# Attention output stored by query and gathered by head in the reload, and two value loads one step earlier

## The chip, the cores and the metric

The kernel runs on one core of one Trainium2 chip. The metric is the device time of one execution in microseconds (us), as the median of several runs. The engines are named as the profile names them: PE is TensorE (PEld its weight loads), DVE is VectorE, ACT is ScalarE, POOL is GpSimd, SP is SyncE, and SPq or ACTq is the sequencer of that engine, which also issues DMAs.

## The reference, cut to what matters

A decoder layer on 64 sequences of 64 tokens with 128 features, float32: self-attention, cross-attention, and a feed-forward part with one shared expert and one of seven routed ones.

```python
p = einsum('bsd,ed->bse', layernorm(x), Wv) + bv       # q = k = v = p, 16 heads of 8
out = softmax(q @ k.T / sqrt(8)) @ v                   # (b, h, s, 8)
out = out.reshape(b, s, h * dk)                        # heads are NOT transposed back
x = x + einsum('bsd,ed->bse', out, Wo) + bo
x = x + cross_attention(layernorm(x), ctx, ctx)        # no projections
x = x + ffn(layernorm(x))                              # shared and routed experts
```

What matters here is the third line. The output of the self-attention has the order (head, query, feature) for a sequence, and it is read again as 64 rows of 128 numbers. A row therefore holds the 8 features of 16 successive queries of one head: row 4h + j has head h and queries 16j to 16j + 15. The kernel's partitions hold queries, with all heads side by side, so this regrouping crosses partitions. The kernel makes it by writing the output to a scratch tensor in DRAM, `attention_out`, and reading it back.

## The kernel before, in words

The 4096 tokens are cut into U = 32 units of 128 tokens, two sequences (b = 0, 1) each. The first phase is a software pipeline over steps t = 0 to 38. In step t the table `LAG` (L223) gives each stage its unit: norm and transposition for unit t, projection and self scores for t - 1, self softmax for t - 2, the stage `out` for t - 3, the stage `q` (output projection, then the cross query and cross scores) for t - 4, cross softmax for t - 5, and so on. `phase_a` (L235) calls each engine's `body` for each step. Steps 0 to 4 have orders of their own (`opening`), and after step 32 every engine but SP has an order written out by hand. The second phase runs the feed-forward part.

The way of the self-attention's output of unit u:

- DVE divides by the softmax sums in `normalise("s", u)` (L1484 to L1491), which writes `on_s` and raises `s_on`. From the second unit on it first waits until both stores of the unit before have landed (`s_out`).
- Two DMAs store it, `store_half` (L283): SP stores sequence 0 (L338), ACT sequence 1 (`second_store`, L1133). Both raise `s_out`. In ACT's order the store stands behind both exponentials of the self softmax (L1250 to L1256), which wait for DVE's subtractions (L1474).
- SP waits for `s_out` of both and issues one reload of 128 rows of 512 bytes into `orow` (L350). It raises `w_rows0` or `w_rows1`, by the unit's parity.
- PE waits for that in `turn_output` (L766), which is the first operation of PE's step u + 4 (L851), and transposes the rows (L771). ACT copies the result (L1181), PE projects it (L776). The last but one unit (30) goes through `turn_last_row` (L894) in the order written out by hand; the last unit needs no way through DRAM.

In one step SP issues, in this order: store, `last_values` in step 33 alone, up to two fills of the routing scratch (`prefill_of_step`, 130 KB each, steps 6 to 31), reload, at most one load of weights, and four loads of cross keys (up to step 31). ACT issues its store, one bulk load in many steps, and two loads of cross values (`cross_values`, L1138) with `ring` slot u % 8 as their target. A load of values moves 64 rows into pieces of 32 bytes, as a store of the attention output does. `last_values` (L327) issues from SP the four value loads of units 30 and 31.

Of the kernel before, what the change touches and what calls it, by code (L numbers as in the profile page):

```python
# [22 lines left out]
P = 128  # L23
D = 128
S = 64
B = 64
H = 16
DK = D // H
NB = P // S
U = B // NB  # L30
# [29 lines left out]
F32 = mybir.dt.float32  # L60
# [6 lines left out]
def build(nc, x, ctxk, ctxv, wv, bv, wo, bo, rw, rb, wup, wdn, ident, hmask, tri, small, tokens, out):  # L67
    ctx = ExitStack()
    with ctx:
# [5 lines left out]
        def sem(name):  # L75
            if name not in sems:
                sems[name] = ctx.enter_context(nc.semaphore(name))
            return sems[name]
# [192 lines left out]
        block = ctx.enter_context(nc.Block())  # L271


        o_dram = nc.dram_tensor("attention_out", (U, NB, H, S, DK), F32, kind="Internal").ap()
        o_rows = o_dram.rearrange("u b h q d -> (u b h q d)").rearrange("(u p c) -> u p c", p=P, c=D)
        hs_dram = nc.dram_tensor("sorted_rows", (SLOTS * P, ROW), F32, kind="Internal").ap()
        hs_halves = hs_dram.rearrange("r (k c) -> (r k) c", k=2)
        hs_tiles = hs_dram.rearrange("(s p) c -> p s c", p=P)
# [3 lines left out]

        def store_half(eng, u, b):  # L283

            load(eng, o_dram[u, b, :, :, :].rearrange("h q d -> q h d"),
                 on["s"][S * b:S * (b + 1), :, :, :].rearrange("p a c d -> p (a c) d"), "s_out")

        @block.sync
        def _(sp):
# [45 lines left out]
            def body(t, u, live):  # L335
                if live("out") and u["out"] < U - 1:
                    sp.wait_ge(sem("s_on"), at(u["out"]))
                    store_half(sp, u["out"], 0)  # L338
                if t == U + 1:
                    last_values(U - 2)  # L340
                    last_values(U - 1)
                for tile in prefill_of_step(t):
                    load(sp, hs_tiles[:, tile, :], nowhere_row[:, :], "prefilled")
                if 6 <= t < 6 + P // H:
                    load(sp, wo_turn[H * (t - 6):H * (t - 5), :, :], wo.rearrange("(q d) e -> q d e", d=DK), "l_turn")
                if live("out") and u["out"] < U - 1:
                    sp.wait_ge(sem("s_out"), 16 * NB * at(u["out"]))
                    if u["out"] >= 2:
                        sp.wait_ge(sem("s_oT"), at(u["out"]) - 2)
                    load(sp, orow[u["out"] % 2][:], o_rows[u["out"], :, :], f"w_rows{u['out'] % 2}")  # L350
                weights_of_step(t)
                for q, half in key_parts(t):
                    keys(t // CHUNK, q, half)
                if t == CHUNK - 1:
                    load(sp, x_all[:, RING:RING + 4, :], xv[:, RING:RING + 4, :], f"l_x{RING}")
                if t == U - 4:
                    load(sp, rb_sb[:], rb.partition_broadcast(P), "l_router")
                if t == U - 3:
                    load(sp, small_sb[:], small.partition_broadcast(P), "l_router")
                if t == U - 2:  # L360
                    load(sp, tok_sb[:], tokens, "l_router")
# [294 lines left out]
        def _(pe):  # L656
# [106 lines left out]

            def turn_output(u):

                pe.wait_ge(sem(f"w_rows{u % 2}"), 16 * (u // 2 + 1))  # L766
                if u == 0:
                    pe.wait_ge(sem("obias"), 1)
                if u >= 1:
                    pe.wait_ge(sem("x_q"), u)  # L770
                nc.tensor.transpose(ps_oT, orow[u % 2][:], id_sb[:]).then_inc(sem("s_oT"), 1)  # L771
# [121 lines left out]

            def turn_last_row(u):  # L894

                pe.wait_ge(sem(f"w_rows{u % 2}"), 16 * (u // 2 + 1))
                nc.tensor.transpose(ps_oT, orow[u % 2][:], id_sb[:]).then_inc(sem("s_oT"), 1)

            def cross_scores_last():
# [1044 lines left out]
```

## Time and profile before

| | us |
|---|---|
| median of 3 runs | 407.66 |
| lowest and highest run | 405.99, 408.55 |
| time of the profiled execution | 406.13 |
| span of the profile in it | 403.9 |

The granted clock of PE is 0.998 of full speed over the span. The profiled execution's own time is 2.2 us more than its span, which is what lies around the program's first and last instruction. A line of the profile names a group of instructions by its line in the code, its engine, its operation and the tiles out<-in.

### The profile page before, as it was taken

How to read it: one execution, taken by the hardware profiler on the slowest of the kernel's cores; microseconds unless marked ns; L12 is line 12 of the kernel's file. 1: busy time of each engine (PE TensorE's matmuls, PEld its weight loads, DVE VectorE, ACT ScalarE, POOL GpSimd, SP SyncE). 2: the span in 40 equal slices, each digit the busy share in tenths (PEclk: the TensorE clock that was granted, in tenths of full speed). 3: DMA queues.
4: the chain of work that ended last, by engine and by line, in shares of the span. 5: the costliest groups of instructions: out<-in, count | busy, mean ns of one | idle time of the engine just before them, and what ended most of it. 6: DMA issues, size and time to landing. Idle time of an engine off the chain costs nothing.

```text
span 403.9 us, 16288 instructions
## 1 busy us (share of the span) xinstructions
PE 393.0 (97%) x5549; PEld 309.9 (77%) x5550; DVE 308.4 (76%) x847; ACT 295.8 (73%) x684; POOL 283.2 (70%) x476
## 2 busy tenths in 40 slices
PE   8989999999999999999999899899999999999996
PEld 5556666666666666666666667799999999999996
DVE  6759999999999999999999786864444454455444
ACT  7568999999999999999999766432224666666651
POOL 8756888888888888888888734467777454444442
PEclk9999999999999999999999999999999999999999
DMA  6254656777777777766554500012223454520001
GB/s 93 59 82 61 99 93 98 138 108 136 111 141 117 125 119 137 137 119 104 68 65 51 54 2 3 0 61 87 87 86 108 111 135 136 138 82 21 30 33 54
DMA packets 176325, 35.22 MB, mean 87 GB/s; under 512 B 145587, under 2 KB 174646, under 8 KB 176256
## 3 DMA queue, kind: packets, MB, share of 16 engines
q1 hardware_dynamic: 71296, 21.43, 24.7%
q10 hardware_dynamic: 102144, 6.81, 16.2%
q0 software_dynamic: 2816, 6.10, 4.3%
q8 instruction: 40, 0.66, 0.7%
q14 instruction: 29, 0.24, 0.2%
HBM read 20.86 MB, written 15.67 MB: 90 GB/s over the span
## 4 chain that ended last, share of the span: by engine, by line
PE 84%; DVE 5%; DMA 4%; issue 2%; ACT 2%; SPq 1%; POOL 1%; ACTq 0%; DVEq 0%; POOLq 0%
PE psum L919 21%; PE psum L672 14%; PE psum L681 14%; PE psum L1026 11%; PE psum L693 9%; PE psum L703 3%; PE psum L771 2%; DMA orow<-attention_out 2%; PE psum L803 2%; PE psum L776 2%; PE psum L810 1%; PE psum L660 1%; PE psum L1068 1%; SPq L198 1%; DVE mx_s L1454 1%
## 5 line engine op out<-in xcount | busy, mean ns | idle before, releaser
L1713 DVE TENSOR_TENSOR gT<-gT,psum 128x384 f32<-128x384 f32 x66 | 36.6, 554 | 65.8 <-ACT gT L1356 40.7
L460 POOL TENSOR_TENSOR k_s<-pT,hmask_sb 128x1024 f32<-128x1024 f32 x32 | 60.9, 1902 | 16.2 <-issue 14.7
L1356 ACT ACTIVATE gT<-psum 128x384 f32<-128x384 f32 x70 | 34.1, 487 | 45.2 <-PE psum L919 36.2
L633 POOL DMA_INDIRECT out<-yrow,token x38 | 37.0, 973 | 40.1 <-DVE yrow L1848 35.4
L1026 PE MATMUL psum<-wdn_sb,gT 128*128 (+1 forms) x420 | 58.3, 276 | 0.7 <-POOL gT L607 0.6
L919 PE MATMUL psum<-fhT,wtile 128*128 128x128 f32 x456 | 57.1, 275 | 0.0
L919 PEld LDWEIGHTS psum<-fhT,wtile 128*128 128x128 f32 x456 | 53.9, 192 | 0.0
L1026 PEld LDWEIGHTS psum<-wdn_sb,gT 128*128 128x128 f32 x420 | 52.4, 192 | 1.3 <-POOL gT L607 1.0
L919 PE MATMUL psum<-hT_all,wup_sb 128*128 128x128 f32 x384 | 48.1, 276 | 1.0 <-ACT gT L1356 1.0
L1454 DVE TENSOR_REDUCE mx_s<-psum 128x16 f32<-128x1024 f32 x33 | 40.4, 1225 | 9.1 <-PE psum L672 6.0
L919 PEld LDWEIGHTS psum<-hT_all,wup_sb 128*128 128x128 f32 x384 | 45.4, 192 | 1.2 <-ACT gT L1356 1.2
L681 PEld LDWEIGHTS psum<-id_sb,pr_x 128*128 128x128 f32 x248 | 27.3, 141 | 24.1 <-ACT pr_x L1118 23.7
L1118 ACT ACTIVATE pr_x<-pr_x,rs 128x512 f32<-128x512 f32 x60 | 40.4, 715 | 3.4 <-DVE pr_x L1466 2.3
L1474 DVE TENSOR_TENSOR pr_s<-psum,mx_s 128x512 f32<-128x512 f32 x64 | 41.8, 658 | 0.0
L1118 ACT ACTIVATE pr_s<-pr_s 128x512 f32<-128x512 f32 x64 | 40.2, 631 | 2.0 <-DVE pr_s L1474 1.7
L1125 ACT COPY prT_s<-psum 128x512 f32<-128x512 f32 x66 | 36.4, 586 | 2.5
L681 PE MATMUL psum<-id_sb,pr_x 128*128 128x128 f32 x248 | 37.4, 280 | 0.5 <-ACT pr_x L1118 0.5
L681 PE MATMUL psum<-id_sb,pr_s 128*128 128x128 f32 x264 | 36.8, 279 | 0.4 <-ACT pr_s L1118 0.3
L1474 DVE TENSOR_TENSOR pr_x<-psum,mx_x 128x512 f32<-128x512 f32 x58 | 37.1, 681 | 0.0
L1125 ACT COPY prT_x<-psum 128x512 f32<-128x512 f32 x62 | 36.7, 595 | 0.1
L1459 DVE TENSOR_REDUCE mx_x<-psum 128x8 f32<-128x512 f32 x56 | 36.0, 685 | 0.4 <-PE psum L672 0.3
L1385 ACT COPY wtile<-wup_sb 128x704 f32 x38 | 29.6, 778 | 7.7 <-issue 7.1
(193 smaller groups left out, 866.9 us busy)
## 6 DMA issues: line engine op xcount, KB each, us to landing
sorted_rows<-nowhere_row SPq DMA_DIRECT2D x38, 130.0 KB, 3.4
ring<-sorted_rows SPq DMA_DIRECT2D x30, 130.0 KB
wup_sb<-in_wup SPq DMA_DIRECT2D x14, 176.0 KB, 2.6
orow<-attention_out SPq DMA_DIRECT2D x31, 64.0 KB
ring<-in_ctxv ACTq DMA_DIRECT2D x60, 32.0 KB, 3.8
cross_keys<-in_ctxk ACTq DMA_DIRECT2D x14, 128.0 KB, 3.3
ring<-cross_keys SPq DMA_DIRECT2D x112, 16.0 KB
rows_all<-in_x ACTq DMA_DIRECT2D x10, 128.0 KB, 3.3
```

Of the source, the lines that this page charges most:

```text
L460: nc.gpsimd.tensor_tensor(k_s[:], pT[:].rearrange("p (b k) -> p b k", b=NB).unsqueeze(2).broadcast_to([P, NB, HG, S]), hmask_sb[:, 0:HG].u ...
L633: pool.indirect_dma_start(out=out, out_offset=bass.IndirectOffsetOnAxis(ap=token[p][:, 0:1], axis=0), in_=yrow[p][:, :], in_offset=None, b ...
L672: last = nc.tensor.matmul(ps_s[k][g][S * b:S * (b + 1), :], q[S * g:S * (g + 1), S * b:S * (b + 1)], keys[S * g:S * (g + 1), b, :, :].rear ...
L681: last = nc.tensor.transpose(ps_s[k][g][:, i * P:(i + 1) * P], pr[k][:, g, 2 * i:2 * i + 2, :].rearrange("p h k -> p (h k)"), id_sb[:])
L693: last = nc.tensor.matmul(ps_wT[k][VW * i:VW * (i + 1), g, S * b:S * (b + 1)], values[:, VW * pair:VW * (pair + 1)], prT[k][:, g, i, S * b ...
L919: return nc.tensor.matmul(ps[p][:, c * P:(c + 1) * P], weights[:, start:start + P], tokens, start=True, stop=True)
L1026: last = nc.tensor.matmul(ps_y[p], gT[place_of(n) if isinstance(n, int) and n < FIRST else p][:, c, :], wdn_sb[:, expert, c, :], start=(c ...
L1118: nc.scalar.activation(pr[k][:, g, :, :], pr[k][:, g, :, :], ACT.Exp, scale=rs[u % 2][:, 0:1] if k == "x" else float(DK) ** -0.5).then_inc ...
L1125: nc.scalar.copy(prT[k][:, g, :, :].rearrange("p i q -> p (i q)"), ps_s[k][g]).then_inc(sem(f"{k}_prT"), 1)
L1454: nc.vector.tensor_reduce(mx[k][:], both(k), AX.X, ALU.max).then_inc(sem(f"{k}_mx"), G)
L1474: nc.vector.tensor_tensor(pr[k][:, g, :, :], scores_of(k, g), mx[k][:, g, :].unsqueeze(2).broadcast_to([P, HG, S]), ALU.subtract).then_inc ...
L1713: nc.vector.tensor_tensor(g, g, ps_up[k][:, 0:CH * P], ALU.mult).then_inc(sem("f_g"), 1)
```

## The change

Three edits. First, `attention_out` gets the order (unit, sequence, query, head, feature). A store then writes 64 rows of 512 bytes, where it wrote 1024 pieces of 32 bytes. Second, the reload becomes two DMAs on SP, one for each sequence, each of which gathers 1024 pieces of 32 bytes; a piece is 8 features of one head and one query, and the 16 pieces of a row lie 512 bytes apart in DRAM. Both raise the same semaphore, so PE waits for twice the count. Third, `last_values` for units 30 and 31 is issued in step 32, behind the reload, where it was issued in step 33, ahead of the reload.

```diff
@@ -271,8 +271,7 @@
-        o_dram = nc.dram_tensor("attention_out", (U, NB, H, S, DK), F32, kind="Internal").ap()
-        o_rows = o_dram.rearrange("u b h q d -> (u b h q d)").rearrange("(u p c) -> u p c", p=P, c=D)
+        o_dram = nc.dram_tensor("attention_out", (U, NB, S, H, DK), F32, kind="Internal").ap()
@@ -282,8 +281,8 @@
         def store_half(eng, u, b):
 
-            load(eng, o_dram[u, b, :, :, :].rearrange("h q d -> q h d"),
-                 on["s"][S * b:S * (b + 1), :, :, :].rearrange("p a c d -> p (a c) d"), "s_out")
+            load(eng, o_dram[u, b, :, :, :].rearrange("q h d -> q (h d)"),
+                 on["s"][S * b:S * (b + 1), :, :, :].rearrange("p a c d -> p (a c d)"), "s_out")
@@ -336,9 +335,6 @@
-                if t == U + 1:
-                    last_values(U - 2)
-                    last_values(U - 1)
                 for tile in prefill_of_step(t):
@@ -347,7 +343,12 @@
-                    load(sp, orow[u["out"] % 2][:], o_rows[u["out"], :, :], f"w_rows{u['out'] % 2}")
+                    for b in range(NB):
+                        load(sp, orow[u["out"] % 2][S * b:S * (b + 1), :].rearrange("p (i d) -> p i d", d=DK),
+                             o_dram[u["out"], b, :, :, :].rearrange("(j i) h d -> h j i d", i=H), f"w_rows{u['out'] % 2}")
+                if t == U:
+                    last_values(U - 2)
+                    last_values(U - 1)
                 weights_of_step(t)
@@ -763,7 +764,7 @@ and @@ -893,7 +894,7 @@
-                pe.wait_ge(sem(f"w_rows{u % 2}"), 16 * (u // 2 + 1))
+                pe.wait_ge(sem(f"w_rows{u % 2}"), 16 * NB * (u // 2 + 1))
```

## Rows read from the trace of the kernel before

**Rows 1.** The page, busy time of each engine and granted clock in 40 slices.

```profile
PE 393.0 (97%) x5549; PEld 309.9 (77%) x5550; DVE 308.4 (76%) x847; ACT 295.8 (73%) x684; POOL 283.2 (70%) x476
...
PEclk9999999999999999999999999999999999999999
```

**Rows 2.** Busy time by stretch: stretch, its us, busy of each engine, clock, DMA share.

```profile
5.90:33.00 27.10, 24.71 (x331) 14.51 (x329) 18.31 (x38) 16.16 (x39) 17.40 (x26) 1.00 0.51 77
...
46.90:224.80 177.90, 177.84 (x3329) 119.53 (x3329) 173.73 (x464) 168.46 (x414) 155.77 (x288) 1.00 0.67 109
224.80:258.00 33.20, 30.05 (x367) 22.30 (x363) 25.36 (x71) 22.45 (x47) 13.24 (x30) 1.00 0.14 15
```

**Rows 3.** The chain that ended last, one steady step: start us, us, what.

```profile
190.91 0.26 PE psum L771
...
196.73 1.02 PE psum L672 x8
197.75 0.26 PE psum L771
```

**Rows 4.** Timeline of a steady step: start us, us, engine, line, operation, tiles.

```profile
189.51 0.28 DVE L1490 TENSOR_TENSOR on_s<-psum,rden_s 128x128 f32<-128x128 f32 x1
189.70 0.68 DVE L1474 TENSOR_TENSOR pr_s<-psum,mx_s 128x512 f32<-128x512 f32 x1
...
190.42 0.64 ACTq L198 DMA_DIRECT2D attention_out<-on_s  x1
190.44 0.58 SPq L198 DMA_DIRECT2D attention_out<-on_s  x1
...
192.90 0.64 ACTq L198 DMA_DIRECT2D ring<-in_ctxv  x1
```

**Rows 5.** Timeline of the next stretch, SP and DVE.

```profile
194.51 0.35 SPq L198 DMA_DIRECT2D orow<-attention_out  x1
194.96 1.34 SPq L198 DMA_DIRECT2D ring<-cross_keys  x4
...
196.35 0.28 DVE L1490 TENSOR_TENSOR on_s<-psum,rden_s 128x128 f32<-128x128 f32 x1
```

**Rows 6.** Waits of 46.9 to 224.8: who waited for whom, us in total, times, longest.

```profile
PEld psum L771 <- DMA orow<-attention_out: 11.4, 14, 0.8
PEld psum L771 <- issue: 9.7, 12, 0.8
...
SPq L198 <- DMA attention_out<-on_s: 54.1, 26, 3.0
```

**Rows 7.** DMA issues, KB each, median us from issue to landing; the whole span.

```profile
wup_sb<-in_wup SPq DMA_DIRECT2D x14, 176.0 KB, 2.6
...
ring<-in_ctxv ACTq DMA_DIRECT2D x60, 32.0 KB, 3.8
...
out<-rows_all SPq DMA_DIRECT2D x2, 64.0 KB, 1.6
```

**Rows 8.** The same of 100 to 200 alone.

```profile
ring<-in_ctxv ACTq DMA_DIRECT2D x30, 32.0 KB, 4.1
```

**Rows 9.** Packets by DMA queue (q1 is SP's, q10 ACT's), 226.2 to 228.2.

```profile
q1 hardware_dynamic: 2238, 0.07, 60.8%
```

**Rows 10.** Packets by DMA queue, 129.2 to 130.6, then 194.4 to 195.4.

```profile
DMA packets 2563, 0.08 MB, mean 61 GB/s; under 512 B 2563, under 2 KB 2563, under 8 KB 2563
...
q10 hardware_dynamic: 608, 0.02, 30.3%
```

**Rows 11.** SP from 217 on, timeline.

```profile
217.18 0.58 SPq L198 DMA_DIRECT2D attention_out<-on_s  x1
220.88 0.35 SPq L198 DMA_DIRECT2D orow<-attention_out  x1
223.53 0.58 SPq L198 DMA_DIRECT2D attention_out<-on_s  x1
224.16 3.57 SPq L198 DMA_DIRECT2D ring<-in_ctxv  x4
```

**Rows 12.** The chain at 227.8, then the timeline with PE's idle time before the line.

```profile
227.85 3.73 DMA orow<-attention_out
...
231.71 0.30 PE L897 MATMUL psum<-id_sb,orow 128*128 128x128 f32 x1 [0.88 <-DMA orow<-attention_out]
```

**Rows 13.** Timeline of the opening, then a piece of the chain there.

```profile
20.07 0.66 ACTq L198 DMA_DIRECT2D attention_out<-on_s  x1
...
26.44 0.33 PE L771 MATMUL psum<-id_sb,orow 128*128 128x128 f32 x1 [0.90 <-DMA orow<-attention_out]
...
29.98 2.94 DMA orow<-attention_out
```

More of the change, by code:

```diff
@@ L894, in turn_last_row @@
             def turn_last_row(u):
-                pe.wait_ge(sem(f"w_rows{u % 2}"), 16 * (u // 2 + 1))
+                pe.wait_ge(sem(f"w_rows{u % 2}"), 16 * NB * (u // 2 + 1))
                 nc.tensor.transpose(ps_oT, orow[u % 2][:], id_sb[:]).then_inc(sem("s_oT"), 1)
```

## The prediction

> **What bounds the kernel now.** I read the page first, then the busy time by stretch, the chain of waits in one step, the timeline of that step, the waits of PE and SP, and last the DMA issues and packets. The page shows PE busy for 393.0 of 403.9 us at full granted clock [rows 1]. By stretch the reader is to see that this isn't an average over slack: from 46.9 to 224.8, 26 steps of 6.84 us, PE is busy for 177.84 of 177.90 us, while the DMA engines are busy for 0.67 of the time [rows 2]. The chain of a steady step is PE alone, and PE's transposition of the reloaded rows (L771) starts at 190.91 and 197.75, 6.84 us apart, right behind the cross scores (L672) [rows 3]. So nothing that the change makes faster can shorten a steady step; it can only lengthen one, if the rows come after PE wants them. What is to gain lies outside: at the first transposition PE is idle for 0.90 us waiting for the reload [rows 13], and at unit 30 for 0.88 us [rows 12]. Together 1.8 us, that is all.
>
> **How much cover the way through DRAM has.** DVE's output ends at 189.51 + 0.28 = 189.79 [rows 4], and PE takes the rows of that unit at 197.75 [rows 3]: 7.96 us. Let D be the time from DVE's end to the landing of the reload; as long as D is under 7.96, the step stays. Before the change the stores go out at 190.42 and 190.44 [rows 4] and SP issues the reload at 194.51 [rows 5], 4.1 us later. The reload's landing is in the chain twice, 2.94 us after its issue [rows 13] and 3.73 us [rows 12]; so D before is up to 4.72 + 2.94 = 7.7, and the waits agree that it is close: in 14 of 26 steps the rows came after PE had finished its last weight load, which is at most 0.8 us ahead of the transposition [rows 6]. That idle time is PEld's, under the running L672, and costs nothing now.
>
> What a miss costs: after a transposition at 190.91 the output that ends at 196.35 + 0.28 = 196.63 [rows 5] belongs to the unit two further on. A unit's round is thus two steps, 5.72 + D, and a step takes (5.72 + D) / 2 once D is over 7.96. A D that is 0.3 us too long costs 0.15 us a step, 4 us over 27 steps.
>
> **Part 1, the store.** ACT's store can't go out earlier: it stands behind the second exponential, which waits for the subtraction that ends at 189.70 + 0.68 = 190.38 [rows 4]. So the later issue stays at 0.6 us behind DVE's end. No row has a store of 64 rows of 512 bytes in this traffic. The nearest are the stores of 128 such rows at the end of the program with nothing beside them, 1.6 us to landing, and the 176 KB weight loads inside the traffic, 2.6 us [rows 7]. I take the middle, 2.1; with 0.6 the reload is issued at 2.7 behind DVE's end, where it was at 4.7. SP's wait for the store, 54.1 us over 26 steps [rows 6], 2.1 each, about disappears; nothing else is late for it, since the key loads behind it have a whole step.
>
> The Trainium skill, "DMA: Bandwidth & Descriptors", section "Specifications", says that below 512 bytes a DMA engine does a read-modify-write. By this rule the store loses a penalty and the reload gets it, for the same 2048 pieces a unit; the rule agrees with a change that moves cost rather than removing it.
>
> **Part 2, the reload.** One issue of 0.35 us becomes two of about 0.6, as the stores and value loads of 1024 pieces take [rows 4]. SP has room for it: in rows 5 it ends its keys at 196.30 with the reload at 194.51; with the reload two us earlier it is done before the next store. For the landing, the nearest row is the load of values, also 1024 pieces of 32 bytes from DRAM to SBUF: 3.8 us to landing over the span [rows 7], 4.1 us in the busiest part [rows 8]. The second gather follows in the same queue. In SP's queue four value loads in a row moved 2238 packets in 2.0 us, 1119 a us [rows 9], so the second lands 1024 / 1119 = 0.9 us behind the first. With 3.8 and 4.1 the pair needs 4.7 to 5.0. D after is 2.7 + 4.7 = 7.4, or 7.7 in the busiest part: as before, and under 7.96 by 0.2 to 0.5. The median leaves room, the single steps not all: I count one step in four as late by 0.2, which costs half of that each, 7 x 0.1 = 0.7 us.
>
> The bounds of the pair: below, as many packets as two queues moved together, 2563 in 1.4 us or 1831 a us [rows 10], so 3.8 - 0.9 + 2048 / 1831 = 4.0 us and D = 6.7, no step late. Above, a value load that runs alone with 608 packets in 1.0 us [rows 10], so 4.1 + 1024 / 608 = 5.8 us, D = 2.7 + 5.8 = 8.5, a miss of 0.54, 0.27 x 27 = 7.3 us. That a piece is now read apart from its neighbours, 512 bytes on, is in no row of the trace. I stay with the value loads in SP's queue, rows 9, for they are the same queue and size.
>
> On the two queues becoming one: the row shows 1119 a us from one queue and 1831 a us from two. The Trainium skill, "DMA: Bandwidth & Descriptors", section "Issuing engines are not separate DMA queues", has it that issuing from several engines saves only the sequencer's time. By this rule the pair would land 0.7 us earlier, D = 6.7 and the steady part would cost nothing; the rows speak against it.
>
> **Part 3, the last values.** In step 33 the four value loads take SP's queue from 224.16 for 3.57 us, up to 227.73, and the reload goes out at 227.85 behind them [rows 11, 12]. Moved, they follow the reload pair of unit 29: store at 217.18, ACT's 0.6 behind, pair issued at 219.8 to 221.1, values to 221.1 + 3.6 = 224.7. The store of unit 30 wants to go at 223.53 [rows 11] and now goes at 224.7, and its queue still holds packets: 6 x 1024 from 221.2 + 1.2 at 1119 a us end at 227.9, at 1831 at 225.8. The store lands 0.4 behind that or 2.1 behind its issue, 226.8 to 228.3; I take 227.6. With little beside it (DMA share 0.14, [rows 2]) the pair takes 4.2, between 4.0 and 4.7, and lands at 231.8, where the old reload landed at 227.85 + 3.73 = 231.58 [rows 12]. So the move takes 3.57 us of issues off the chain and gets nothing for it: the longer reload eats it. I take +0.2, between -0.9 (PE's idle time gone) and +1.4 (store at 228.3, pair 4.7).
>
> **The opening.** Unit 0: ACT's store goes at 20.07 [rows 13], lands at 22.2, the pair at 26.9 with 4.7, where PE started at 26.44. The 256 KB load behind the old reload now comes after the pair. Unit 1: stores at 26.45, landing 28.5, pair 33.2 or 32.5 with 4.0, against 29.98 + 2.94 = 32.92. I take +0.3 for both, between -0.9 and +1.0.
>
> **Sum.** 0.7 + 0.2 + 0.3 = +1.2 us. Against the profiled execution's 406.1 us (span 403.9 and 2.2 around it) that is 407.3. The median of the runs is 407.7, 1.5 above the profiled one, so for a median I say 408.9 (407.7 + 1.2).
>
> **The rivals.** A, the gather outlasts its cover (slower): scattered reads of 32 bytes in one queue beside ACT's value loads. Its place is the wait of L771 in every steady step. It decides from a pair longer than 7.96 - 2.7 = 5.3 us; at the upper bound of 5.8 it costs 7.3 us, with the 0.5 of the ends 407.7 + 7.8 = 415.5. For it: no row has reads that lie apart, the cover has 0.2 to 0.5 us left, and ACT's value loads (192.90, [rows 4]) fall beside the gather. Against it: DMA engines are idle for a third of the time [rows 2].
> B, a small gain: the store lands in 1.6 and the pair in 4.0. Then both idle times of PE shrink, together at most -1.8 us: 405.9 in the median, 404.3 for the profiled one. Against it: the pair's price.
> C, the end alone is worse: values and gather in one queue hold back the store of unit 30, +1.4 there, and the opening +1.0, with the steady part 0.7: +3.1, 410.8. For it: the four issues now stand in front of a store that the chain runs through.
>
> **How the numbers follow.** The forecast has 0.43, A 0.27, B 0.16, C 0.14. A measurement of this kernel can tell about 1% (4.1 us) from no change. Forecast, B and C lie within it, A over it except for its mildest part (0.02); I leave 0.03 for a gain over 1%, which no row offers, taken from B. So faster 0.03, same 0.71, slower 0.26. The range goes from B's 405.9 to A's 415.5, rounded up to 416.
>
> **What would show it.** Right: SP's reload goes out about 2.1 us behind the later store, L771 stays 6.84 us apart, PE is busy for all of the steady stretch, and the idle time before L897 is near 0.9. Wrong: idle time of PE (not only PEld) before L771 in most steps, the steady stretch longer than 178 us, or cross scores no longer directly ahead of L771 in the chain. If the store still takes 4 us with its 512-byte rows, its cost was traffic and not its pieces, and D goes to 9.4 and the kernel to some 427.

## The result, and the profile after

The changed kernel takes 422.91 us (median of 4 runs, 420.66 to 425.35), the one before 407.13 us in the same session (405.99 to 408.55). The ratio is 1.039, with a 95% interval of 1.034 to 1.045: slower, beyond the upper end of the range. The profiled execution took 420.66 us, span 418.4.

The page of the kernel after, busy time, clock, two of the queues and the chain's shares:

```profile
PE 397.1 (95%) x5549; PEld 312.8 (75%) x5550; DVE 308.8 (74%) x847; ACT 297.1 (71%) x684; POOL 283.8 (68%) x476
...
PEclk9989999999999999999999969999999999999999
...
q1 hardware_dynamic: 101552, 21.43, 26.9%
q10 hardware_dynamic: 72384, 6.81, 12.6%
...
PE 54%; DMA 21%; SPq 15%; DVE 3%; issue 3%; ACT 2%; POOL 1%; DVEq 0%; POOLq 0%; ACTq 0%
```

Beside [rows 1], PE has 4.1 us more of busy time and 14.5 us more of span. Two slices have a lower clock, which had none before. The chain is now DMA and SP's sequencer (SPq) for 36% of the span.

Busy time by stretch, the kernel after; columns as in [rows 2]:

```profile
5.90:33.00 27.10, 23.59 (x294) 14.68 (x293) 15.47 (x32) 15.01 (x35) 16.47 (x25) 0.94 0.47 72
...
46.90:224.80 177.90, 170.12 (x3215) 114.69 (x3217) 166.42 (x446) 161.94 (x398) 148.88 (x273) 1.00 0.65 108
```

PE was busy for 177.84 us of the steady stretch [rows 2] and is now for 170.12. The DMA engines are no busier than they were (0.65, before 0.67), so by this mean it isn't their throughput that ran out.

Waits of 46.9 to 224.8, kernel after:

```profile
PEld psum L772 <- DMA orow<-attention_out: 28.0, 24, 2.6
...
PE psum L772 <- DMA orow<-attention_out: 7.7, 10, 1.8
```

The second line is the loss; before there was no such line [rows 6]. The steady chain of [rows 3] was PE alone. After, from 142 to 151 us (start, us, what):

```profile
142.22 3.18 DMA attention_out<-on_s
145.40 0.02 issue
145.42 0.55 SPq L198
145.97 0.04 issue
146.01 4.27 DMA orow<-attention_out
150.28 0.04 issue
150.32 0.33 PE psum L772
```

Ahead of 142.22 the chain runs twice through seven SPq pieces and the landing of a store, from 128.13 to 135.18 and on to 142.22, 7.05 and 7.04 us. So the circle store, landing, reload pair, weights, keys, next store on SP sets the pace. One turn of it in the timeline of SP, kernel after:

```profile
159.37 1.47 SPq L198 DMA_DIRECT2D orow<-attention_out  x2
160.88 1.64 SPq L198 DMA_DIRECT2D wdn_sb<-in_wdn  x1
162.56 2.88 SPq L198 DMA_DIRECT2D ring<-cross_keys  x4
165.49 0.47 SPq L198 DMA_DIRECT2D attention_out<-on_s  x1
```

And the output that this store carries, from the timeline of all engines:

```profile
162.65 0.28 DVE L1491 TENSOR_TENSOR on_s<-psum,rden_s 128x128 f32<-128x128 f32 x1
163.57 0.51 ACTq L198 DMA_DIRECT2D attention_out<-on_s  x1
```

DVE ends at 162.93 and ACT stores its half 0.64 later, as forecast. SP stores its half 2.56 us after DVE's end. In the kernel before, the turn of the same unit has its reload at 152.58, the weight load at 152.95 (0.43 us) and the keys at 153.43 (1.45 us); SP was done at 154.88, DVE at 155.53, and the store went out at 155.56. The next turn of the kernel before, which is at the time of the one above:

```profile
160.73 0.33 SPq L198 DMA_DIRECT2D orow<-attention_out  x1
161.10 0.44 SPq L198 DMA_DIRECT2D wdn_sb<-in_wdn  x1
161.58 2.68 SPq L198 DMA_DIRECT2D ring<-cross_keys  x4
164.30 0.58 SPq L198 DMA_DIRECT2D attention_out<-on_s  x1
```

The weight load's issue took SP 0.44 us there, and 1.64 behind the gather pair. The store of this turn was late before the change too, though: DVE's output ended at 162.37 and it went out at 164.30, 1.93 us later, behind key issues of 2.68 us. Before, that is the one late turn among units 10 to 23, the next worst being 0.92; after, eleven of the 14 are later than 1.1 us. The held weight load is no single case either. Issues in 130 to 205 by tile, first the kernel before, then after (ns min/median/max; first and last start in us):

```profile
L198 SPq DMA_DIRECT2D wdn_sb<-in_wdn x6: 428/435/441, 153.0 to 188.2; - x6
...
L198 SPq DMA_DIRECT2D wup_sb<-in_wup x3: 433/433/433, 132.9 to 146.9; - x3
```

```profile
L198 SPq DMA_DIRECT2D wdn_sb<-in_wdn x6: 661/1675/1895, 160.9 to 197.4; - x6
L198 SPq DMA_DIRECT2D wup_sb<-in_wup x4: 738/1401/1632, 132.5 to 153.7; - x4
```

Where the time went, by the start of PE's transpositions (before, then after): unit 0 26.44, then 28.11; unit 3 46.79, then 49.77; unit 29 224.81, then 235.58; unit 30 231.71, then 244.26; end of the span 403.88, then 418.41. So 3.0 us come by unit 3, 7.8 in units 4 to 29, 1.8 at unit 30 and 2.0 behind it.

The opening, chain of waits after:

```profile
22.92 5.14 DMA orow<-attention_out
28.06 0.04 issue
28.11 0.47 PE psum L772
28.58 1.71 PE psum L682 x8
```

Two stretches of the kernel after with PE's clock halved (columns as in [rows 2]):

```profile
28.00:31.40 3.40, 3.29 (x34) 2.96 (x37) 0.54 (x2) 1.71 (x4) 0.00 (x0) 0.50 0.22 30
...
243.10:249.90 6.80, 5.62 (x24) 3.31 (x25) 2.14 (x9) 1.98 (x5) 1.80 (x5) 0.50 0.14 23
```

In the first, the eight matmuls of L682 take 1.71 us, where the chain has 0.96 for eight of them at full clock. Each stretch came with a longer idle time of PE ahead of the transposition, 2.20 us and 2.66 us, than the 0.90 and 0.88 of before [rows 12, 13]. The clock fell from 2.4 to 1.2 GHz inside that idle time, 0.1 us before its end in the first and 1.2 us in the second.

The end of the phase, timeline of SP after, which answers to [rows 11]:

```profile
233.06 4.47 SPq L198 DMA_DIRECT2D ring<-in_ctxv  x4
237.58 0.67 SPq L198 DMA_DIRECT2D attention_out<-on_s  x1
240.83 1.28 SPq L198 DMA_DIRECT2D orow<-attention_out  x2
```

DVE's output of unit 30 ends at 234.27 (its row starts at 233.98 and has 0.29); SP's store waits 3.3 us for the four value issues, which the change moved ahead of it.

### The profile page after: what moved, and what is told of

Read it like the earlier page. It is cut to its first block, busy times and chain, and to the rows that moved or that the text cites. A ratio compares the mean times of both kernels' runs of the same rounds, so it can differ in the third digit from the quotient of the medians.

```text
span 418.4 us, 16319 instructions
## 1 busy us (share of the span) xinstructions
PE 397.1 (95%) x5549; PEld 312.8 (75%) x5550; DVE 308.8 (74%) x847; ACT 297.1 (71%) x684; POOL 283.8 (68%) x476
## 3 DMA queue, kind: packets, MB, share of 16 engines
q1 hardware_dynamic: 101552, 21.43, 26.9%
q10 hardware_dynamic: 72384, 6.81, 12.6%
## 4 chain that ended last, share of the span: by engine, by line
PE 54%; DMA 21%; SPq 15%; DVE 3%; issue 3%; ACT 2%; POOL 1%; DVEq 0%; POOLq 0%; ACTq 0%
PE psum L920 21%; SPq L198 15%; DMA attention_out<-on_s 14%; PE psum L1027 10%; DMA orow<-attention_out 6%; PE psum L682 5%; PE psum L673 5%; PE psum L694 4%; PE psum L661 1%; PE psum L704 1%; PE psum L1069 1%; ACT pr_s L1119 1%; PE psum L772 1%; DVE mx_s L1455 1%; PE psum L711 1%
## 5 line engine op out<-in xcount | busy, mean ns | idle before, releaser
L682 PEld LDWEIGHTS psum<-id_sb,pr_x 128*128 128x128 f32 x248 | 27.4, 141 | 23.8 <-ACT pr_x L1119 23.5
L682 PE MATMUL psum<-id_sb,pr_x 128*128 128x128 f32 x248 | 37.3, 280 | 0.5 <-ACT pr_x L1119 0.5
L682 PE MATMUL psum<-id_sb,pr_s 128*128 128x128 f32 x264 | 36.9, 281 | 0.4 <-ACT pr_s L1119 0.3
```

The lines of the kernel that those rows point to most:

```text
L682: last = nc.tensor.transpose(ps_s[k][g][:, i * P:(i + 1) * P], pr[k][:, g, 2 * i:2 * i + 2, :].rearrange("p h k -> p (h k)"), id_sb[:])
```

## The experiments

The table has means over units 10 to 23, read from the timeline and the landings of each DMA: how long after DVE's end the later store goes out, from there to the reload's issue ("lands"), the reload's issue to its landing, their sum D, and SP's time from the reload's issue to the end of the last issue of its step ("SP block"; the last key load, or the tiny loads). The step is the distance of PE's transpositions. One traced execution stands behind each row, and two of the same kernel differ by 0.15 us a step (7.38 and 7.53), so smaller differences than that say nothing. Most experiments ran on chips where the kernel before takes 420 us. The extra time, some 12 us, lies behind the attention phase: the changed kernel is at unit 30 at 244.26 in its first trace and at 247.15 in its second, and ends at 418.41 and 433.15. Why is open. So each ratio is with the kernel before on its own chip. The rows "two plain reloads" and "two in pieces" ran where it takes 408.

| kernel | ratio [95%] | later store | lands | reload lands | D | SP block | step |
|---|---|---|---|---|---|---|---|
| before | 1 | 0.78 | 3.94 | 2.39 | 7.11 | 2.52 | 6.86 |
| after | 1.039 [1.034, 1.045] | 1.62 | 2.62 | 4.44 | 8.68 | 4.47 | 7.38 |
| after, again | 1.041 [1.034, 1.048] | 1.53 | 2.44 | 4.71 | 8.68 | 4.40 | 7.53 |
| two tiny loads | 1.003 [1.000, 1.007] | 0.94 | 3.73 | 2.76 | 7.43 | 3.07 | 6.93 |
| plain reload | 0.991 [0.987, 0.996] | 0.64 | 2.45 | 2.59 | 5.68 | 2.39 | 6.85 |
| two plain reloads | 0.994 [0.990, 0.998] | 0.64 | 2.52 | 3.53 | 6.69 | 3.41 | 6.85 |
| two in pieces | 1.017 [1.010, 1.024] | 1.51 | 2.42 | 4.16 | 8.09 | 4.31 | 7.14 |
| weights late | 1.011 [1.006, 1.016] | 0.82 | 2.43 | 4.70 | 7.95 | 3.76 | 7.04 |
| mixed ways | 1.019 [1.014, 1.024] | 1.09 | 3.25 | 3.89 | 8.23 | 3.65 | 7.23 |
| stores on ACT | 1.037 [1.031, 1.043] | 1.18 | 3.16 | 4.02 | 8.36 | 4.09 | 7.35 |
| keys first | 1.024 [1.017, 1.030] | 0.64 | 3.70 | 4.48 | 8.82 | - | 7.58 |
| one gather by ACT | 1.115 [1.108, 1.121] | 0.64 | 2.41 | 3.94 | 6.99 | 2.87 | 8.30 |
| weights late, values behind | 1.006 [1.002, 1.010] | 0.69 | 2.29 | 4.66 | 7.63 | 3.23 | 6.92 |

**Parts of the change undone or done alone.** First the changed kernel with the values back in step 33, ahead of the reload.

```diff
+                if t == U + 1:
+                    last_values(U - 2)
+                    last_values(U - 1)
...
-                if t == U:
-                    last_values(U - 2)
-                    last_values(U - 1)
```

> The changed kernel with the value loads of units 30 and 31 back in step 33, ahead of the reload (third edit undone). Theory 1 (SP's sequencer is what the gathers block: DMAs issued behind the pair wait their turn, so SP's next store goes out late): in the changed kernel SP's store of unit 30 went out 3.3 us behind DVE's end, behind the four value loads. Back in step 33 it goes out within 0.6 us, but the pair then stands behind 3.6 us of value issues. Transposition 29 to 30, 8.7 us in the changed kernel and 6.9 before, becomes 7.3 to 8.2; the kernel 0.5 to 1.5 us faster than the changed one, about 421 to 422. Theory 2 (the store and the pair are themselves too long, whenever they are issued): no change of the steady part, and the end as in the changed kernel or worse, 423. Neither expects the steady part to change.

Measured 1.029 [1.025, 1.033]. Both stores of unit 30 go out within 0.39 us of DVE's end again. About 1% comes back; the rest stays, so the moved values are the smaller part. (Its traced execution, 438.23 us, was the longest of its four, so its steps aren't in the table.) Now that part alone, on the kernel before (the same lines the other way round).

> The kernel before with the third edit alone: value loads of units 30 and 31 in step 32 behind the reload. The single reload of unit 30 no longer stands behind 3.6 us of issues. Theory 1: SP's store of unit 30 goes out late instead (by about 0.5 to 1.5 us, the values end issuing at about 224.7), so of PE's 0.88 us idle at L897 about half goes; the kernel -0.5 to +0.5 against before, 407. Theory 2: nothing is late for issuing, the whole 0.88 us goes: 406.3. A result over 409 would say that the values' place makes a good part of the loss by itself.

0.9985 [0.9955, 1.0015]: no difference. The store of unit 30 goes at 1.15 behind DVE and the single reload lands in 2.00 us. The move costs only together with the gathers, whose pieces stand in the queue as well. Third, both stores issued by ACT.

```diff
-                if live("out") and u["out"] < U - 1:
-                    sp.wait_ge(sem("s_on"), at(u["out"]))
-                    store_half(sp, u["out"], 0)
...
+                store_half(act, u, 0)
```

> The changed kernel with both stores issued by ACT, one behind the other, none by SP. Theory 1: the later store goes out about 1.1 us behind DVE's end in every unit (1.6 on average and up to 2.75 in units 10 to 23 of the changed kernel), so with landing 2.6 and pair 4.4 D is 8.1 or less and steps of units 10 to 23 take 6.9 to 7.0 us where they took 7.38; the end gains too, since SP's blocked store was 3.3 us late. In all 413 to 416. Theory 2: the path is as long as before with a store half a microsecond later than the best, so steps stay at 7.3 to 7.4 and the kernel at 420 or more.

Measured 1.037 [1.031, 1.043], as the change. The store is off SP and goes out at 1.18 in every unit, as forecast, yet the gain didn't come. The landing took 3.16 us where 2.6 were expected, the second store's issue alone being 1.12, so D is 8.36. And DVE's output itself ends later: 6.07 us behind the transposition of two units before, in the mean of units 10 to 23, where the changed kernel has 5.78. The formula gives (6.07 + 8.36) / 2 = 7.2 for these; why DVE is later is open. ACT queue, timeline of this run:

```profile
160.64 0.50 ACTq L198 DMA_DIRECT2D attention_out<-on_s  x1
...
161.18 1.12 ACTq L198 DMA_DIRECT2D attention_out<-on_s  x1
```

The theory in its first form, take the store off SP and all is well, fell. Fourth, weights and keys issued ahead of the wait and the pair.

```diff
+                weights_of_step(t)
+                for q, half in key_parts(t):
+                    keys(t // CHUNK, q, half)
...
-                weights_of_step(t)
-                for q, half in key_parts(t):
-                    keys(t // CHUNK, q, half)
```

> The changed kernel with SP's loads of weights and cross keys issued ahead of the wait for the stores, so that nothing but the pair stands at the end of SP's step. Theory 1: SP's time of waiting for the store takes them, the next store goes out on time (0.0 to 0.6 us, later one 0.6), and steps of units 10 to 23 fall from 7.38 towards 6.9 to 7.1; the pair itself may land up to 1 us later behind their packets. In all 413 to 418. Theory 2: the pair lands later behind more packets and nothing is gained: 422 or more.

1.024 [1.017, 1.030]: some two fifths of the loss go, less than expected. Timeline of SP in this run, behind a pair at 162.28:

```profile
164.66 1.28 SPq L198 DMA_DIRECT2D attention_out<-on_s  x1
165.98 1.23 SPq L198 DMA_DIRECT2D sorted_rows<-nowhere_row  x2
167.25 0.46 SPq L198 DMA_DIRECT2D wdn_sb<-in_wdn  x1
167.75 1.48 SPq L198 DMA_DIRECT2D ring<-cross_keys  x4
169.32 1.50 SPq L198 DMA_DIRECT2D orow<-attention_out  x2
```

It tells more than its time. The weight load, with no pair right ahead of it, is issued in 0.46 us again. The store that follows the pair takes 1.28 here, but 0.48 in the other 13 of units 10 to 23, where up to 3.3 us lie between the pair's issue and it. The later store is on time in all 14, at 0.64. But the pair now waits for SP's own issues: 3.70 us from store to pair, for a store that lands in 2.60, so D is 8.82. The lateness has moved from the store to the pair, and in this traced execution (433.46 us, the longest of its four) the steady stretch is no better than the change's, PE being busy for 167.10 of 177.90 us. Where the gain of the median lies is not shown.

**The change again, and the queue unloaded.** First the change as it is:

> The changed kernel unchanged, as a control beside the others of this call. All theories: as on record, 1.03 to 1.05 times the kernel before; steps of units 10 to 23 at 7.3 to 7.7 us, transposition 30 at 244 to 248.

1.041 [1.034, 1.048]: the change costs the same on this chip. Next, the 20 weight loads moved behind the phase.

```diff
-                weights_of_step(t)
+            for t in range(W_STEP, W_STEP + 2 * E + 2 * CH):
+                weights_of_step(t)
```

> The changed kernel with SP's 20 loads of expert weights issued behind the first phase (SP waits there for 75 us) and none in steps 8 to 27. Theory 1, now narrower (SP's sequencer is full: store 0.5, wait for the landing 2.3 to 2.8, pair 1.3, the DMA behind it blocked for 1.1 to 1.7, keys 1.4 to 2.9, together over 6.84 us, so SP's next store is late): without the weight load the keys are the blocked ones and SP ends about 0.5 to 1 us earlier; the later store goes out at 0.6 to 0.9 behind DVE's end (1.6 in the changed kernel), D falls to 7.7 to 8.0 and steps of units 10 to 23 to 6.85 to 7.0. The first phase ends 5 to 7 us earlier than in the control, while the second may lose a little to the weights beside its scatters. Theory 2 (pair and store too long by themselves): later store as in the control, steps 7.3 or more. Theory 3 (traffic: fewer bytes in flight make store and pair themselves faster): landing and pair shrink by over 0.5 us each while the lateness stays.

1.011 [1.006, 1.016]. With one issue less in the block, the store goes out at 0.82 and D falls by 0.73 us, while store and pair land as they did (2.43 and 4.70, in the change again 2.44 and 4.71): fewer bytes in flight made neither faster. Steady stretch of this run:

```profile
46.90:224.80 177.90, 173.92 (x3294) 117.02 (x3285) 169.82 (x457) 165.44 (x407) 152.04 (x278) 1.00 0.59 87
```

The rows are the same, the gathers are the same, and PE lacks 3.9 us of the 177.84 of before, where the changed kernel in its second trace lacks 9.8 (busy for 168.04) and in its first 7.7. So the block on SP is a cause of its own. It also shows that the hold isn't a matter of the weight load: now the first key load stands behind the pair, and its issue takes 1.05 us in the mean of units 10 to 23 (0.56 to 2.14), where the median of all key loads of the changed kernel in 130 to 205 is 0.31. Next, the stores of the change with one plain reload of 128 rows of 512 bytes.

```diff
-                    for b in range(NB):
-                        load(sp, orow[...][S * b:S * (b + 1), :].rearrange("p (i d) -> p i d", d=DK),
-                             o_dram[u["out"], b, :, :, :].rearrange("(j i) h d -> h j i d", i=H), ...)
+                    load(sp, orow[u["out"] % 2][:], o_rows[u["out"], :, :], f"w_rows{u['out'] % 2}")
```

> The changed kernel's stores with one reload of 128 rows of 512 bytes; the rows come back in the order of queries, so the regrouping by head is left out. This prices the store part alone. All theories: store landing 2.1 to 2.6, reload 2.0 to 2.4, D 5.0 to 5.5, steps 6.84, PE busy throughout. Theory 1 and 2 expect the ends to gain: transposition 0 at 25.9 (PE was idle 0.9 before), no fall of the clock after it, and transposition 30 at 230.8 to 231.2, so 1 to 2 us faster than the kernel before. If instead it is slower than before, the stores or the moved values carry a part of the loss.

0.991 [0.987, 0.996], faster than before. The store in whole rows is good for what it was meant to be: landed in 2.45 instead of 3.94, D 5.68. But the steady stretch gets nothing from it, as forecast:

```profile
46.90:224.80 177.90, 177.84 (x3332) 119.75 (x3332) 173.77 (x465) 168.51 (x414) 155.93 (x288) 1.00 0.53 109
```

Then the second gather issued by ACT.

```diff
-                    for b in range(NB):
-                        load(sp, orow[...][S * b:S * (b + 1), :]...
+                    reload_half(sp, u["out"], 0)
...
+                if live("out"):
+                    second_reload(u["out"])
```

> The changed kernel with the gather of sequence 1 issued by ACT (units 0 to 29), which first waits for both stores; SP gathers sequence 0 alone. Theory 1: SP's queue loses 0.66 us of issue and half of what blocks it, the later store goes out at 0.6 to 0.8, steps of units 10 to 23 fall to 6.85 to 7.1 unless ACT's wait and issue (0.6 us more a step on an engine that is busy for 6.5 of 6.84 us) give a part of it back, up to 0.3 a step. Theory 2 (two gathers in one queue land too late, in themselves): the pair's landing falls from 4.4 to 3.8 or less and that is where the gain is; the lateness of SP's store stays at 1.6 if SP's queue is not the cause.

1.115 [1.108, 1.121], the worst of all. On SP things went as theory 1 has it: the later store goes out at 0.64, the weight load behind the one gather takes 0.66 us, and D is 6.99, under the cover. What costs is ACT. ACT must wait for the landed stores before it issues, and its next exponentials stand behind that wait. Waits of 46.9 to 224.8:

```profile
PE psum L687 <- ACT pr_x L1124: 27.2, 22, 2.5
ACT pr_x L1124 <- issue: 24.0, 13, 2.8
```

**A little more load on SP, and mixtures.** Two loads of four bytes more on SP at the end of steps 8 to 31 of the kernel before.

```diff
+                if 8 <= t < U:
+                    for n in range(2):
+                        load(sp, idle_sb[:, 2 * t + n:2 * t + n + 1], bv[0:1].unsqueeze(0), "l_first")
```

> The kernel before with two DMAs of 4 bytes on SP at the end of each of the steps 8 to 31, behind the keys; they move nothing, but each takes SP some 0.4 us to issue. Theory 1 (SP's sequencer has a budget of one step, and its loop of store, landing, reload and issues is what went over it): the loop before is 4.0 to 4.1 from the later store to the reload, then 0.35 + 0.43 + 1.6, about 6.5 to 6.9; with 0.8 more it is 7.3, so SP's store goes out late (1 us and more) and steps of units 10 to 23 take 7.1 to 7.4 us, the kernel 1.01 to 1.03 times the one before. Theories 2 and 3 (the gathers' own length, traffic): nothing changes, 6.86 a step, 1.000.

1.003 [1.000, 1.007]. They added 0.55 us to the block (0.28 each, where I had 0.4) and 0.07 to the step. So half a microsecond more on SP costs the kernel before next to nothing, and plain issues are cheap. Then the values behind the reload in step 33, in the kernel before:

> The kernel before with the value loads of units 30 and 31 left in step 33, but behind the reload of unit 30. Theory 1: store and reload of unit 30 both go out at once (store at 223.5, reload at 226.9 to 227.6, landed at 229 to 230), so PE's 0.88 us idle before L897 goes; the values land at about 232 and are wanted at 243. 0.5 to 0.9 us faster than before, 0.998. If the value loads' place were of no matter, 1.000.

0.9991 [0.9963, 1.0019]: nothing gained. The four issues were hardly on the chain: the reload goes out 4.06 us behind DVE's end, where it went out 4.34 behind it with them ahead, for it waits for its stores anyway. And it lands in 3.59 with them behind it, hardly sooner than 3.73. Then a mixture meant to beat both: sequence 0 stored in pieces and reloaded plain, sequence 1 the new way.

```diff
+            if b == 0:
+                load(eng, o_head[u, :, :, :].rearrange("h q d -> q h d"), ...)
+            else:
+                load(eng, o_query[u, :, :, :].rearrange("q h d -> q (h d)"), ...)
```

> A version meant to beat both: sequence 0 goes the old way (SP stores pieces, reload of 64 whole rows), sequence 1 the new way (ACT stores whole rows, which is the later store, and SP gathers); the last values as in h1_values_behind. One gather of 1024 pieces and one reload take SP 0.95 us where the pair takes 1.26, and block less behind them. Theory 1: later store at 0.6, landing 2.5 to 3.0 (4.0 before), gather 3.5 to 3.8 (2.4 for the old reload), D 6.7 to 7.3, steps 6.84, no wait of PE for rows in the steady part; at the ends 0 to 1.5 us gained: 0.996 to 1.000. If a single gather already overfills SP's queue, the later store is over 0.8 and steps over 6.9: 1.005 or more.

1.019 [1.014, 1.024]. Half of the gather brings half of the loss. Last, the changed kernel with weights late and the values behind the pair in step 33.

```diff
-                if t == U:
+                if t == U + 1:
...
-                weights_of_step(t)
+            for t in range(W_STEP, W_STEP + 2 * E + 2 * CH):
```

> The changed kernel with the weights behind the first phase (as g1_weights_late) and the values of units 30 and 31 in step 33 behind the reload pair. Theory 1: as g1 up to unit 29; the store of unit 30 goes out within 0.6 us where it was 3.6 late, its pair is issued ahead of the values, so transposition 29 to 30 takes 6.9 to 7.2 us (8.0 in g1) and the fall of the clock behind it is gone. 1 to 2.5 us faster than g1: 1.005 to 1.009 times the kernel before. Theory 2: the pair's own length keeps it at 8 us.

1.006 [1.002, 1.010]. Timeline of SP at its end:

```profile
228.19 0.48 SPq L198 DMA_DIRECT2D attention_out<-on_s  x1
231.06 1.25 SPq L198 DMA_DIRECT2D orow<-attention_out  x2
232.35 4.06 SPq L198 DMA_DIRECT2D ring<-in_ctxv  x4
```

SP's store goes 0.03 us after DVE's end (227.87 + 0.29) and 2.9 ahead of the pair; from unit 29 to unit 30 this kernel needs 5.96 us, where the change with the weights late needs 8.03 and the change itself 8.68. The 2.1 us between the first two, which differ in nothing else but the chip that they ran on, are the price of the third edit, shown from its own side.

**What holds SP's issues.** Open was whether it is that there are two DMAs, that they are of 32-byte pieces, or that the pieces are read 512 bytes apart. First the plain reload in two DMAs of 64 rows.

```diff
-                    load(sp, orow[u["out"] % 2][:], o_rows[u["out"], :, :], f"w_rows{u['out'] % 2}")
+                    for b in range(NB):
+                        rows = slice(S * b, S * (b + 1))
+                        load(sp, orow[u["out"] % 2][rows, :], o_rows[u["out"], rows, :], ...)
```

> The plain reload of the earlier experiment issued as two DMAs of 64 rows of 512 bytes, so that the number of SP's DMAs is the change's and the pieces are not (the regrouping is left out). Theory 'number of DMAs': one more issue and one more transfer in SP's queue holds the weight and key loads behind it; reload's issue to the last key issued then rises from 2.4 us towards 3.5, and the ratio goes from 0.991 to 1.00 or more. Theory 'pieces': SP's issues behind a plain pair go through as before, at most 0.4 us more, 2.8 us; the weight load's issue stays near 0.43 us and the ratio is 0.99.

0.994 [0.990, 0.998]. Then two DMAs of 1024 pieces, written 64 bytes apart in `orow` but read from 256 bytes that lie together.

```diff
+                        load(sp, orow[...][:].rearrange("p (i t d) -> p i t d", t=2, d=DK)[:, :, b, :],
+                             o_rows[u["out"], :, :].rearrange("p (t i d) -> t p i d", t=2, d=DK)[b], ...)
```

> As the run with two plain reloads, but each of the two writes 128 rows of 8 pieces of 32 bytes, 1024 pieces, read from 256 bytes that lie together in DRAM (the regrouping is left out): the change's number of DMAs and of pieces, without its reads 512 bytes apart. Theory 'pieces in SP's queue': the issue of the weight load behind the pair is held for 1.1 us or more, reload's issue to the last key issued 4 us or more, and the ratio is that of the change, 1.03 to 1.04. Theory 'reads that lie apart': it is the gather's addresses in DRAM that make it slow; then this run is as the plain pair, ratio 0.99 to 1.00, the reload landed in under 3.5 us.

1.017 [1.010, 1.024]. Issues of weight loads in 130 to 205, first two plain, then two in pieces:

```profile
L198 SPq DMA_DIRECT2D wdn_sb<-in_wdn x6: 589/609/707, 151.8 to 186.5; - x6
...
L198 SPq DMA_DIRECT2D wup_sb<-in_wup x3: 586/587/683, 131.5 to 145.4; - x3
```

```profile
L198 SPq DMA_DIRECT2D wdn_sb<-in_wdn x6: 582/819/1803, 158.9 to 195.3; - x6
L198 SPq DMA_DIRECT2D wup_sb<-in_wup x4: 1057/1336/2149, 131.2 to 152.0; - x4
```

And the steady stretch of the second, 46.9 to 222:

```profile
46.90:222.00 175.10, 169.48 (x3153) 114.13 (x3149) 164.15 (x441) 159.92 (x393) 147.10 (x268) 0.99 0.65 109
```

A second plain DMA lengthens the block by 1.0 us and the weight load's issue from 0.43 to about 0.6, and costs PE nothing (in the same stretch PE is busy for 175.05 of 175.10 us). With 32-byte pieces in the same two DMAs, the issue behind them takes 0.8 to 1.3 us in the median and PE loses 5.6 us. Over units 10 to 23 it is 1.35 us in the mean here and 1.34 in the change: the pieces are what holds SP, whether their addresses lie apart or not. My expectation of this run was too high in its time, 1.03 to 1.04. This run has the values in step 32 as the change has, so 2.2 points are between them (1.017 and 1.039), and the traces tell where. Units 4 to 29 take 178.0 us before, 185.4 here and 185.8 in the change, 189.7 in its second trace: the steady loss is there with the pieces alone, or most of it. The opening costs 0.7 us up to unit 3 here and 3.0 in the change; the step to unit 30 is 6.77 and 8.68; behind it this run loses nothing and the change 2.0 us. That part comes with the reads that lie apart, if it is not the chip or that the pieces lie on 128 rows here and not on 64; the runs don't separate these.

No version that keeps the regrouping beat the kernel before by more than its interval; the nearest are the two that only move the values, 0.9985 and 0.9991.

## Why the prediction was wrong

**What bounds the kernel: right.** PE alone sets the steady step and has nothing to gain. The plain reload shows it best: D falls from 7.11 to 5.68, and PE's busy time in the stretch is 177.84 before and after.

**Cover and the price of a miss: right, if it is worked out unit by unit.** With D = 8.68 the formula (5.72 + D) / 2 gives 7.20, the trace has 7.38. The same gap stands in the other rows of the table that lose time (7.04 for a D of 7.95, where the formula gives 6.84). A step can come late but never early, so single long values count that the mean of D hides. The traces bear this out. Let each transposition start at the later of two times, 6.84 us after the last one or 5.78 + 0.04 + D after the one two before, with 5.78 for DVE's output and 0.04 from landing to PE as the trace after has them: the measured D's of units 10 to 23, of which 11 are over 7.96, give a step of 7.38. For weights late they give 7.04, for two in pieces 7.13, as measured (7.04, 7.14), for the change's second trace 7.43, where 7.53 was measured. D before was 7.11 in the mean of these units and 7.38 at most, less than the 7.7 that I took from its landing in the opening.

**Part 1, the step that failed.** "So the later issue stays at 0.6 us behind DVE's end", and in part 2 "SP has room for it". It went out at 1.62 in the mean and 2.56 in the turn shown. The store's landing was 2.62 where I had 2.1, which is the smaller miss. I counted SP's room as the sum of issue durations in the trace of before, with 0.6 for each gather. Each gather's own issue is indeed 0.6; what I left out is that the DMA behind them takes longer to issue. Over units 10 to 23 the block went from 2.52 to 4.47 us: 0.95 of it is the pair's own issue, 0.33 before and 1.28 after, which I had counted, and 0.91 the load behind it, 0.43 before and 1.34 after, which I had not. So a turn of SP (store lands 2.62, block 4.47, and the store's own issue inside the former) is 7.1 us, over the step of 6.84. Why the issue is held is not shown. The trace of before had two signs, unread. The value loads in a row take 3.57 us for four issues of 1024 pieces, 0.89 each [rows 11], where one of them alone on ACT takes 0.64 [rows 4]. And the room itself was read from a turn with short key issues, 1.34 us [rows 5]; in the turn with 2.68, shown above, the later store was 1.93 us late already.

**Part 2, the gather: right.** The pair lands 4.44 us after its first issue, forecast 4.7 to 5.0 (bounds 4.0 to 5.8). Later store 1.62, landing 2.62 and pair 4.44 make 8.68; with 0.6 in the first place D would have been 7.66, under 7.96, as forecast. The later store alone thus puts the mean of D over the cover; weights late, with 0.82 there and 4.70 for the pair, has D 7.95 and still loses 1.1%.

On the two rules of the Trainium skill, "DMA: Bandwidth & Descriptors". By "Specifications" the penalty of short pieces moves from store to reload. The trace agrees with a move: the two queues' shares were 24.7% and 16.2% of 403.9 us before, 165 us together, and are 26.9% and 12.6% of 418.4 after, 165 again. The plain store lands in 2.6 us, that of pieces in 3.9. By "Issuing engines are not separate DMA queues" several engines save only the sequencer's time, and the pair should land in 4.0. It took 4.44 and 4.71 from one queue, and 3.94 with the second gather issued by ACT. What mattered was the other half of that sentence: the sequencer's time was the scarce thing, and I had counted only the gathers' own issues of it.

**Part 3, the values: wrong in size.** Forecast were a store 1.2 us late and +0.2 in all. The four value issues took 4.47 us instead of 3.57, from 233.06, and the store was 3.3 us late; the step to unit 30 cost 1.8 us more than before, and PE's wait of 2.66 us brought the half clock behind it, 2.0 us more. Together that is 3.8 against a bound of +1.4. The other term was wrong as well: the move was to take 3.57 us of issues off the chain, and the run with the values behind the reload shows that only 0.3 us of them were on it.

**The opening: wrong in size.** Forecast +0.3, at most +1.0; it was +1.7 at unit 0 (the pair needed 5.8 us, from its first issue at 22.28 to 28.06) and +3.0 by unit 3, with the first stretch of half clock in it. The forecast had 4.7 us for that pair; why it took 5.8 is open. Two plain reloads come at 26.11 there, 0.3 ahead of the kernel before, and show no such stretch.

**The rivals.** A had the direction and the place, a wait of L772 in the steady steps, with a chance of 0.27. It had the wrong cause, the pair's landing (over 5.3 us; it was 4.44), with 7.3 us for the steady part at most and 0.5 for the ends. The steady part cost 7.8, so that A's figure for it came close by luck, and the opening and the end 6.7 more. C, the end alone, came true beside it. Of the signs that I named, all three wrong ones are there: PE idle before L772, a stretch with 170.12 of 177.90 us busy, and SPq in the chain where the cross scores stood. The store of whole rows landing faster was right. One sum in the chances is off by 0.01: from the shares given, no change is 0.72 and slower 0.25.

## What to carry to other kernels

Add up one turn of a DMA-issuing engine as you would that of a computing one: its waits, the landings that it waits for, and its issues; and price an issue by the row of the DMA that stands behind a transfer of many pieces, not by that transfer's own. Put nothing urgent right behind two or more transfers of 1024 small pieces in the same queue, neither a store nor a load. Before you shorten a store, ask which wait ends last: here it was PE, and a D shorter by 1.4 us was worth 0.9%, none of it in the steady stretch; unit 30 is reached 1.7 us sooner (230.01, before 231.71).

## What the runs showed of the hardware

- The issue of a DMA isn't one price. In the mean of units 10 to 23 a weight load took SP 0.43 us behind one plain reload, 0.59 behind two, 0.66 behind one gather of 1024 pieces, 1.35 behind two DMAs of 1024 32-byte pieces and 1.34 behind the two gathers (0.66 to 1.90); it took 0.46 when it stood ahead of the gathers.
- Nothing of this is seen in the DMA engines' share, 0.67 and 0.65 over the steady stretch, and 0.65 also in the held issue shown, 160.88 to 162.52: an issue can be held while the engines are idle for a third of the time.
- PE's clock was at half for 3.4 and 6.8 us behind idle times of 2.20 and 2.66 us; behind those of 0.90 and 0.88 it stayed full in the kernel before. The length of one idle time doesn't settle it: in the run "two in pieces" the clock stayed full behind 2.26 us (up to 178.22).
- The same kernel takes different times on different chips: the one before took 407 to 408 us in two sessions and 420 in three others. The changed kernel, traced in both kinds, differed by 2.9 us up to unit 30 and by some 12 behind it; why is open.
